# State-space stage of a one-core kernel: the step size is folded into the x rows on GpSimd, the chunk's four weighted gram products become one, and a third convolution tile moves from TensorE to ScalarE and VectorE taps

## The chip, the cores and the metric

One Trainium2 chip, one core of it. The metric is the device time of one execution in microseconds (us), measured on that core; lower is better. The engines are TensorE (PE, its weight loads PEld), VectorE (DVE), ScalarE (ACT), GpSimd (POOL) and the DMA queue (SP).

## What is computed

Eight sequences of 512 rows of 128 numbers go through an attention block, a mixture of 16 experts, a state-space block, and the experts again. The change lies in the state-space block, whose core is:

```python
zxbcdt = einsum('bld,ed->ble', u, W_in)            # z, x, B, C, dt
dt = softplus(dt + dt_bias)
conv = conv_b
for w in range(4):                                 # causal, per channel
    conv = conv + xp[:, w:w + L, :] * conv_w[:, w]
xBC = silu(conv)                                   # 512 channels: x (256), B (128), C (128)
dtx = dt[..., None] * x
h = h * exp(dt * A) + outer(dtx, B)                # step by step over the 512 rows
y = h @ C + x * D
g = y * silu(z); g = g * rsqrt(mean(g * g) + eps) * norm_w
out = g @ W_out.T
```

## The kernel before, in words

The program is written by hand: each engine has its own instruction list, and counting semaphores (`M["..."]` for this block) order them. Around the block lie the attention stage, the first expert stage and, behind it, the second expert stage; they are not changed except for a few set-up instructions.

The recurrence is done in chunks: a sequence (batch b, eight of them) has four chunks c of 128 rows. For a chunk, `front` on PE makes the product of B and C rows (bank 0), transposes x and B to row order (bank 1), and sums the log decays (bank 2). ACT copies bank 1 to `xb_tok` (`xb_out`) and exponentiates bank 2 into `segs` (`seg_exp`: four heads of 128x128). DVE (`grams`) masks the product into `cb`, multiplies the last column of `segs` by the step size (`to_end`), and makes for each of the four heads `gram` = segs * dt * cb. PE (`back`) adds into bank 3 the skip term, the term of the carried state, and gram times `xb_tok`; then it makes the chunk's state from `xw`, the x rows weighted by `to_end` on POOL (`weigh`). DVE takes y from bank 3 (`ys`), POOL gates it (`gate`), ACT squares it (`square`), POOL makes the scale (`rms`, two small operations), DVE applies it (`norms`), and PE transposes it (`g_turn`) through bank 5, which ACT empties (`gT_out`).

The next batch's inputs are made in between: `u_turn` and `u_low`, then the projections with the causal convolution of width 4. The 512 channels are four tiles. Two of them (`DVE_TILES`, B and C) are projected once on PE (`project_in`), ACT makes the first tap with the bias (`conv_first`), and DVE adds three taps (`conv_taps_of`), each one pass over 128x511 and fewer elements. The other two (`PE_TILES`, x) are convolved on PE: `conv` runs the split product for each of four shifts, 12 matmuls of 512 columns, against weights that hold the taps (`tapT`). ACT copies out the first of these (`conv_out`) and applies silu to the second straight from PSUM (`xs_last`). The banks are few: bank 7 holds, in turn, the turned rows, tile 0's projection, the first convolution, and the second half of z. `softplus` on DVE is a chain of 15 small operations on 128x16 numbers, which ends with `dt_a`, the step sizes and their products with A.

A step of `skew_pairs` does batch i's chunks (`second`), batch i+1's inputs (`first`), the output projection of batch i-1 (`third`), and parts of the router of batch i-2 (`fourth`). There are nine steps, from -1 (inputs only) to 7 (no inputs). Each engine's order in a step is written out by hand, for instance on DVE:

```python
            def step(i, odd, first, second, third, fourth):
...
                if second:
                    states(i, 1)
                    ys(i, odd, 1)
...
                    grams(i, odd, 2)
                if first:
                    softplus(i + 1, 1 - odd)
                if second:
                    ys(i, odd, 2)
```

An engine takes its instructions in this order and no other, so a wait at the head of one holds all that stand behind it.

## Time and profile before

| | us |
|---|---|
| median of 3 runs | 880.06 |
| lowest and highest run | 880.0, 883.94 |
| the profiled execution, its own time | 880.15 |
| its span in the trace | 878.4 |
| TensorE busy | 783.9 |
| VectorE busy | 670.9 |
| ScalarE busy | 552.8 |
| GpSimd busy | 215.9 |
| the nine steps of the state-space block | about 354.75 to 669.93 |

The span runs from the first to the last instruction in the trace; the device time has 1.7 us around it. Busy times are sums over all stages, and the stages have different limits: a step of the state-space block takes 37.6 to 38.8 us, of which PE is busy about 32 and DVE about 29, so no engine is full there, and which wait ends last has to be read in the step.

### The profile page before, as it was taken

The numbers are of one execution on the slowest core, as the hardware profiler recorded it, in microseconds if no ns is written. First come the engines' busy times: TensorE is split into PE (matmuls) and PEld (weight loads), VectorE is DVE, ScalarE is ACT, GpSimd is POOL, SyncE is SP. The second block draws the span as 40 slices with busy tenths as digits, with TensorE's granted clock in tenths as the row PEclk, the third lists the DMA queues.
The fourth block names the chain that finished last, engine by engine and source line by source line (L and its number), as shares of the span: only waits on it lengthen the run. The fifth ranks groups of instructions, "written<-read, shape, count | busy, mean of one in ns | idle before, by whom it ended". The sixth has DMA issues, their size and how long they took to land.

```text
span 878.4 us, 14762 instructions
## 1 busy us (share of the span) xinstructions
PE 783.9 (89%) x3912; PEld 617.2 (70%) x3912; DVE 670.9 (76%) x1610; ACT 552.8 (63%) x934; POOL 215.9 (25%) x383
## 2 busy tenths in 40 slices
PE   6879997999999999687888979798887899999998
PEld 4656775777777877566776867676665677777776
DVE  3488887878888888585777878687756988888886
ACT  4565656777778776635545363554624877777784
POOL 2235454001000000133545454464534100000000
PEclk9999999899999999998999999999987999999999
DMA  8000002545555452000000000000003445556552
GB/s 229 1 1 3 4 2 86 173 160 181 181 173 182 172 170 72 1 0 1 1 1 2 2 3 1 3 0 2 2 1 122 168 171 185 182 190 194 186 176 69
DMA packets 28113, 75.87 MB, mean 86 GB/s; under 512 B 4323, under 2 KB 8862, under 8 KB 28062
## 3 DMA queue, kind: packets, MB, share of 16 engines
q1 hardware_dynamic: 27908, 75.30, 25.8%
q8 instruction: 19, 0.31, 0.1%
q14 instruction: 32, 0.26, 0.1%
q10 hardware_dynamic: 154, 0.00, 0.0%
HBM read 72.66 MB, written 2.62 MB: 86 GB/s over the span
## 4 chain that ended last, share of the span: by engine, by line
PE 56%; DVE 15%; issue 14%; ACT 6%; POOL 6%; DMA 1%; DVEq 0%; POOLq 0%; SPq 0%; ACTq 0%
PE ps L1442 7%; PE ps L1461 7%; PE ps L1462 6%; PE ps L1463 6%; PE ps L1443 6%; PE ps L1444 6%; DVE conv_acc L1112 3%; PE ps L1613 3%; POOL rt_small L389 2%; PE ps L1439 2%; PE ps L1297 2%; DVE gram L1167 1%; DVE xn L1057 1%; DVE t L911 1%; POOL g L483 1%
## 5 line engine op out<-in xcount | busy, mean ns | idle before, releaser
L684 ACT ACTIVATE s_ring<-ps,b1T 128x512 f32<-128x512 f32 x256 | 172.8, 688 | 85.7 <-PE ps L1463 84.6
L1072 DVE SCALAR_TENSOR_TENSOR s_ring<-s_ring,top_col,r_all 128x1024 f32<-128x1024 f32 x128 | 165.6, 1294 | 64.2 <-ACT s_ring L684 60.1
L1038 DVE TENSOR_TENSOR s_lo<-s_ring,s_hi 128x1024 fp32r<-128x1024 f32 x128 | 156.1, 1219 | 0.0
L672 ACT ACTIVATE s_hi<-s_ring 128x1024 fp32r<-128x1024 f32 x128 | 134.4, 1050 | 1.4 <-DVE s_ring L1072 1.4
L1461 PE MATMUL ps<-ffn_hi,w_hi 128*128 (+1 forms) x256 | 104.8, 409 | 2.0 <-issue 2.0
L1442 PE MATMUL ps<-s_hi,w_hi 128*128 128x512 f32 x256 | 103.4, 404 | 1.4 <-DVE s_lo L1038 1.4
L1462 PE MATMUL ps<-ffn_lo,w_hi 128*128 (+1 forms) x256 | 102.3, 400 | 0.0
L1463 PE MATMUL ps<-ffn_hi,w_lo 128*128 (+1 forms) x256 | 102.3, 400 | 0.0
L1443 PE MATMUL ps<-s_lo,w_hi 128*128 128x512 f32 x256 | 101.4, 396 | 0.0
L1444 PE MATMUL ps<-s_hi,w_lo 128*128 128x512 f32 x256 | 101.3, 396 | 0.0
L457 POOL TENSOR_TENSOR ramp<-upto,dt_a 128x512 f32<-128x512 f32 x32 | 33.4, 1046 | 156.7 <-DVE dt_a L1153 156.7
L1442 PEld LDWEIGHTS ps<-s_hi,w_hi 128*128 128x128 f32 x256 | 48.1, 188 | 25.6 <-issue 12.1
L1461 PEld LDWEIGHTS ps<-ffn_hi,w_hi 128*128 128x128 f32 x256 | 49.2, 192 | 12.7 <-issue 2.3
L1463 PEld LDWEIGHTS ps<-ffn_hi,w_lo 128*128 128x128 f32 x256 | 48.8, 191 | 12.1
L1462 PEld LDWEIGHTS ps<-ffn_lo,w_hi 128*128 128x128 f32 x256 | 48.9, 191 | 10.8
L1444 PEld LDWEIGHTS ps<-s_hi,w_lo 128*128 128x128 f32 x256 | 48.1, 188 | 11.6
L1443 PEld LDWEIGHTS ps<-s_lo,w_hi 128*128 128x128 f32 x256 | 48.2, 188 | 10.5
L483 POOL TENSOR_TENSOR g<-y,zs 128x256 f32<-128x256 f32 x32 | 23.7, 741 | 124.7 <-DVE y L1195 63.0
L1112 DVE SCALAR_TENSOR_TENSOR conv_acc<-ps,conv_taps,conv_acc 128x511 f32<-128x511 f32 (+2 forms) x48 | 35.2, 748 | 10.3 <-ACT conv_acc L714 9.1
L1167 DVE SCALAR_TENSOR_TENSOR gram<-segs,dt_a,cb 128x128 f32<-128x128 f32 x128 | 39.5, 369 | 0.1
L911 DVE TENSOR_SCALAR t<-X,rt_mv,rt_small 128x128 f32<-128x128 f32 (+1 forms) x64 | 31.3, 549 | 8.7 <-POOL rt_small L404 8.7
L1578 PEld LDWEIGHTS ps<-xb_tok,gram 128*128 128x128 f32 x256 | 33.9, 197 | 2.3 <-DVE gram L1167 1.1
(232 smaller groups left out, 1602.3 us busy)
## 6 DMA issues: line engine op xcount, KB each, us to landing
r_all<-route_dram SPq DMA_DIRECT2D x128, 512.0 KB, 3.7
out_dram<-X SPq DMA_DIRECT2D x8, 256.0 KB, 4.1
X<-in_L_attn_a_x_dram SPq DMA_DIRECT2D x1, 1792.0 KB, 9.4
w_rows<-in_L_ffn_mlp_w_dram SPq DMA_DIRECT2D x1, 1024.0 KB, 12.6
route_dram<-route_cols SPq DMA_DIRECT2D x64, 8.0 KB, 1.4
route_rows<-route_dram SPq DMA_DIRECT2D x16, 32.0 KB, 3.4
in_rows<-in_L_attn_b_W_in_dram SPq DMA_DIRECT2D x1, 384.0 KB
X<-in_L_attn_a_x_dram SPq DMA_DIRECT2D x1, 256.0 KB, 2.6
```

What stands on the lines that cost most here:

```text
L672: eng.activation(s_hi[:, q % NR, :, :], s_ring[:, q % NR, :, :], ACT.Copy).then_inc(F["hi"], 1)
L684: eng.activation(s_ring[:, q % NR, e % 2, :], bank(e % 4), ACT.Silu, bias=b1T[:, e:e + 1], scale=ALPHA).then_inc(F["act"], 1)
L1038: eng.tensor_tensor(s_lo[:, q % NR, :, :], s_ring[:, q % NR, :, :], s_hi[:, q % NR, :, :].bitcast(F32), ALU.subtract).then_inc(F["lo"], 1)
L1072: eng.scalar_tensor_tensor(out=s_ring[:, q % NR, :, :], in0=s_ring[:, q % NR, :, :], scalar=top_col[:, 0:1], in1=r_all[:, q % NR, :, :], o ...
L1112: eng.scalar_tensor_tensor(out=conv_acc[:, j, s:], in0=bank(7 - k)[:, 0:SEQ - s], scalar=conv_taps[:, j, CONV_W - 1 - s:CONV_W - s], in1=c ...
L1167: eng.scalar_tensor_tensor(out=gram[:, c % 2, h, :], in0=segs[:, c % 2, h, :], scalar=dt_a[:, par, 0, c, h:h + 1], in1=cb[:, c % 2, :], op ...
L1442: eng.matmul(bank(6), w2_hi[:, e, :], hi, start=False, stop=False)
L1443: eng.matmul(bank(6), w2_hi[:, e, :], lo, start=False, stop=False)
L1444: mm = eng.matmul(bank(6), w2_lo[:, e, :], hi, start=False, stop=(e == NE - 1))
L1461: eng.matmul(bank(e % 4), w1_hi[:, e, :], ffn_hi[:, b, :], start=True, stop=False)
L1462: eng.matmul(bank(e % 4), w1_hi[:, e, :], ffn_lo[:, b, :], start=False, stop=False)
L1463: eng.matmul(bank(e % 4), w1_lo[:, e, :], ffn_hi[:, b, :], start=False, stop=True).then_inc(F["h"], 1)
```

## The change

Three things are changed.

First, the step size is multiplied into the x rows: POOL makes `xdt` = xb_tok * dt for every chunk (`step_x`, one more POOL operation per chunk, placed ahead of `weigh` or, for the last chunk, behind `gate` of the third), and `xw` is made from `xdt` and the last column of `segs`. `to_end` is gone.

Second, `gram` no longer holds dt, so that DVE makes the four heads in one product of 128x512, with `cb` repeated over the heads. PE multiplies it with `xdt`, for which it now waits.

Third, `PE_TILES` is `(1,)` and `DVE_TILES` is `(2, 3, 0)`: the first x tile is projected once on PE into bank 7 (where `conv(0)` stood), ACT makes its first tap (where `conv_out` stood), and DVE its three other taps, between `grams` of the third chunk and `softplus`. The second half of z, which uses bank 7 next, waits for them. In the set-up, one tap tile less and one projection tile more is turned and split.

```diff
-PE_TILES = (0, 1)
-DVE_TILES = (2, 3)
+PE_TILES = (1,)
+DVE_TILES = (2, 3, 0)
+TILE_BANK = (7, 6, 7)
...
+            def step_x(b, par, c):
+                n = NT * b + c
+                wait(eng, M["xb"], n + 1)
+                wait(eng, M["dt"], b + 1)
+                wait(eng, M["y_ps"], n - 1)
+                wait(eng, M["xw"], (NT - 1) * b + max(c - 1, 0))
+                eng.tensor_tensor(xdt[:, c % 2, :].rearrange("s (h p) -> s h p", h=NH),
+                                  xb_tok[:, c % 2, 0:2, :].rearrange("s j (h p) -> s (j h) p", p=HD),
+                                  dt_a[:, par, 0, c, :].unsqueeze(2).to_broadcast([P, NH, HD]),
+                                  ALU.mult).then_inc(M["xdt"], 1)
...
                 if second:
                     gate(i, odd, 1)
                     rms(i, 1)
+                    step_x(i, odd, 2)
                     weigh(i, odd, 2)
                     gate(i, odd, 2)
+                    step_x(i, odd, 3)
                 if first:
                     ramps(i + 1, 1 - odd, 0)
...
             def grams(b, par, c):
...
-                for h in range(NH):
-                    eng.scalar_tensor_tensor(out=gram[:, c % 2, h, :], in0=segs[:, c % 2, h, :],
-                                             scalar=dt_a[:, par, 0, c, h:h + 1], in1=cb[:, c % 2, :], op0=ALU.mult,
-                                             op1=ALU.mult).then_inc(M["gram"], 1)
+                eng.tensor_tensor(gram[:, c % 2, :, :], segs[:, c % 2, :, :],
+                                  cb[:, c % 2, :].unsqueeze(1).to_broadcast([P, NH, P]), ALU.mult).then_inc(M["gram"], 1)
...
                 if first:
+                    conv_taps_of(i + 1, 2)
                     softplus(i + 1, 1 - odd)
...
             def z_proj(b, k):
                 if k == 0:
-                    wait(eng, M["conv"], 6 * b + 6)
+                    wait(eng, M["conv"], 9 * b + 6)
                 else:
-                    wait(eng, M["raw"], b + 1)
+                    wait(eng, M["conv"], 9 * b + 9)
...
-                wait(eng, M["gram"], NH * (n + 1))
+                wait(eng, M["xdt"], n + 1)
+                wait(eng, M["gram"], n + 1)
                 for h in range(NH):
                     mm = eng.matmul(bank(3)[:, h * HD:(h + 1) * HD], gram[:, c % 2, h, :],
-                                    xb_tok[:, c % 2, h // 2, (h % 2) * HD:(h % 2 + 1) * HD], start=False, stop=(h == NH - 1),
+                                    xdt[:, c % 2, h * HD:(h + 1) * HD], start=False, stop=(h == NH - 1),
                                     skip_group_check=True)
...
                 if first:
-                    conv(i + 1, 0)
+                    project_in(i + 1, 2)
```

How the instructions stand on VectorE in the middle of a step, from the third chunk's gram to the same chunk's y, before (`dt_tmp` and `dt_a` are softplus):

```order
L1159 TENSOR_TENSOR cb<-ps,upto 128x128
L1162 TENSOR_TENSOR to_end<-segs,dt_a 128x4
L1167 SCALAR_TENSOR_TENSOR gram<-segs,dt_a,cb 128x128 x4
L1138 TENSOR_SCALAR dt_tmp<-dt_tmp 128x16
L1139 RECIPROCAL dt_tmp<-dt_tmp 128x16
```

and after the change, at the same place:

```order
L1170 TENSOR_TENSOR cb<-ps,upto 128x128
L1174 TENSOR_TENSOR gram<-segs,cb 128x512
L1123 SCALAR_TENSOR_TENSOR conv_acc<-ps,conv_taps,conv_acc 128x511
L1123 SCALAR_TENSOR_TENSOR conv_acc<-ps,conv_taps,conv_acc 128x510
L1123 SCALAR_TENSOR_TENSOR conv_acc<-ps,conv_taps,conv_acc 128x509
L1149 TENSOR_SCALAR dt_tmp<-dt_tmp 128x16
L1150 RECIPROCAL dt_tmp<-dt_tmp 128x16
```

Five instructions of the gram have become one, and three whole-row taps now stand ahead of softplus and of all that follows it, the third chunk's y among them.

GpSimd from the second chunk's gate to the next batch's first ramp, before:

```order
L483 TENSOR_TENSOR g<-y,zs 128x256
L488 TENSOR_TENSOR g_rs<-g_ss,eps 128x1
...
L491 TENSOR_TENSOR g_rs<-g_rs,mhalf 128x1
...
L467 TENSOR_TENSOR xw<-xb_tok,to_end 128x256
...
L473 TENSOR_TENSOR state_d<-state,decay 128x256
L483 TENSOR_TENSOR g<-y,zs 128x256
...
L457 TENSOR_TENSOR ramp<-upto,dt_a 128x512
```

and after:

```order
L495 TENSOR_TENSOR g<-y,zs 128x256
L500 TENSOR_TENSOR g_rs<-g_ss,eps 128x1
...
L503 TENSOR_TENSOR g_rs<-g_rs,mhalf 128x1
...
L468 TENSOR_TENSOR xdt<-xb_tok,dt_a 128x256
L479 TENSOR_TENSOR xw<-xdt,segs 128x256
...
L485 TENSOR_TENSOR state_d<-state,decay 128x256
L495 TENSOR_TENSOR g<-y,zs 128x256
...
L468 TENSOR_TENSOR xdt<-xb_tok,dt_a 128x256
...
L458 TENSOR_TENSOR ramp<-upto,dt_a 128x512
```

The third chunk's `xdt`, for which PE waits, stands behind the second chunk's gate and rms, and the fourth chunk's behind the third chunk's gate.

## Rows read from the trace of the kernel before

**Rows 1.** The page, part 1: busy us of the engines.

```profile
PE 783.9 (89%) x3912; PEld 617.2 (70%) x3912; DVE 670.9 (76%) x1610; ACT 552.8 (63%) x934; POOL 215.9 (25%) x383
```

**Rows 2.** Windows: busy us per engine, granted clock; three steps, one piece.

```profile
479.24:518.08 38.84, 33.76 (x188) 28.18 (x188) 29.09 (x110) 19.58 (x41) 18.26 (x34) 0.91 0.01 2
518.08:555.84 37.76, 31.96 (x187) 26.51 (x188) 29.40 (x110) 19.51 (x41) 19.36 (x34) 1.00 0.01 3
594.19:631.75 37.56, 31.97 (x188) 26.55 (x188) 29.03 (x108) 19.43 (x41) 18.86 (x34) 1.00 0.01 1
...
511.10:514.50 3.40, 3.40 (x9) 2.59 (x9) 2.28 (x17) 3.01 (x4) 2.85 (x9) 0.51 0.00 0
```

**Rows 3.** Timeline of TensorE, step 4: start, us, line, tiles, count [idle before].

```profile
538.93 0.47 PE L1490 MATMUL ps<-uT,tapT 128*128 128x512 f32 x1
...
541.80 0.61 PE L1570 MATMUL ps<-skip_diag,xs 128*128 128x128 f32 x4
542.68 1.00 PE L1578 MATMUL ps<-xb_tok,gram 128*128 128x64 f32 x8
548.59 0.41 PE L1603 MATMUL ps<-ident,gn 128*128 128x128 f32 x2 [1.37 <-ACT gT L794]
555.25 0.30 PE L1358 MATMUL ps<-ident,rt_w 128*128 128x128 f32 x1 [1.07 <-ACT gT L794]
```

**Rows 4.** Timeline of VectorE, step 4.

```profile
522.43 1.82 DVE L1057 TENSOR_SCALAR xn<-X,ln_mv,ln_rs 128x128 f32 x4
...
532.57 4.54 DVE L1112 SCALAR_TENSOR_TENSOR conv_acc<-ps,conv_taps,conv_acc 128x511 f32<-128x511 f32 x6 [1.23 <-ACT conv_acc L714]
...
540.30 1.13 DVE L1167 SCALAR_TENSOR_TENSOR gram<-segs,dt_a,cb 128x128 f32<-128x128 f32 x4
541.35 0.16 DVE L1138 TENSOR_SCALAR dt_tmp<-dt_tmp 128x16 f32<-128x16 f32 x1
545.24 0.17 DVE L1153 TENSOR_TENSOR dt_a<-dt_a,neg_A 128x16 f32<-128x16 f32 x1
```

**Rows 5.** Timeline of ScalarE and GpSimd, step 4.

```profile
531.76 0.78 ACT L714 ACTIVATE conv_acc<-ps,cols,conv_taps 128x512 f32<-128x512 f32 x1 [5.37 <-PE ps L1492]
539.62 0.74 POOL L483 TENSOR_TENSOR g<-y,zs 128x256 f32<-128x256 f32 x1 [3.06 <-DVE y L1195]
540.47 0.42 ACT L787 ACTIVATE g_sq<-g 128x256 f32<-128x256 f32 x1 [2.56 <-POOL g L483]
541.41 0.55 POOL L491 TENSOR_TENSOR g_rs<-g_rs,mhalf 128x1 f32<-128x1 f32 x1 [0.16 <-POOL g_rs L488]
541.92 0.61 POOL L467 TENSOR_TENSOR xw<-xb_tok,to_end 128x256 f32<-128x256 f32 x1
546.29 0.78 POOL L483 TENSOR_TENSOR g<-y,zs 128x256 f32<-128x256 f32 x1 [3.19 <-DVE y L1195]
548.07 0.37 ACT L794 ACTIVATE gT<-ps 128x256 f32<-128x256 f32 x1
```

**Rows 6.** Grouped instructions: prices of one two-input VectorE product.

```profile
L1038 DVE TENSOR_TENSOR s_lo<-s_ring,s_hi 128x1024 fp32r<-128x1024 f32 x128 | 156.1, 1219 | 0.0
L1205 DVE TENSOR_TENSOR X<-ps,X 128x512 f32<-128x512 f32 x4 | 2.8, 692 | 8.5 <-PE ps L1613 8.5
```

**Rows 7.** Timeline of VectorE: grams beside GpSimd work, and xn behind it.

```profile
372.83 2.28 DVE L1167 SCALAR_TENSOR_TENSOR gram<-segs,dt_a,cb 128x128 f32<-128x128 f32 x4
...
446.14 2.14 DVE L1057 TENSOR_SCALAR xn<-X,ln_mv,ln_rs 128x128 f32<-128x128 f32 x4 [0.17 <-POOL ln_rs L451]
```

**Rows 8.** Timeline of step -1: VectorE's softplus, first and last.

```profile
361.69 0.18 DVE L1138 TENSOR_SCALAR dt_tmp<-dt_tmp 128x16 f32<-128x16 f32 x1 [0.28 <-ACT dt_tmp L754]
364.70 0.18 DVE L1153 TENSOR_TENSOR dt_a<-dt_a,neg_A 128x16 f32<-128x16 f32 x1
```

**Rows 9.** Timeline of the last step, third chunk: GpSimd and TensorE.

```profile
650.96 0.54 POOL L491 TENSOR_TENSOR g_rs<-g_rs,mhalf 128x1 f32<-128x1 f32 x1
651.15 1.97 PE L1578 MATMUL ps<-xb_tok,gram 128*128 128x64 f32 x8 [0.73 <-DVE gram L1167]
```

**Rows 10.** Timeline of the set-up: TensorE's wait behind it.

```profile
55.98 3.67 PE L1297 MATMUL ps<-xnT,qT 128*128 128x512 f32 x8 [1.35 <-DVE dtT L1013]
```

More of the change, by code:

```diff
@@ L155, in build @@
             xb_tok = own("xb_tok", [P, 2, 3, P])
-            to_end = own("to_end", [P, 2, NH])
+            xdt = own("xdt", [P, 2, DI])
             xw = own("xw", [P, 2, DI])
@@ L224, in build @@
         M = {n: sem("ssm_" + n) for n in (
-            "stats", "aggr", "rstd", "xn", "uT_ps", "uT", "u_lo", "cv_ps", "tap", "conv", "raw", "xs", "z_ps",
+            "stats", "aggr", "rstd", "xn", "uT_ps", "uT", "u_lo", "cv_ps", "tap", "conv", "xs", "z_ps",
             "z_raw", "zs", "dt_ps", "dt_x", "dt_m", "dt_u", "log", "dt", "a", "dk_ps", "decay", "ramp", "cb_ps", "cb",
-            "xb_ps", "xb", "seg_ps", "segs", "gram", "end", "xw", "st_ps", "state_d", "state", "y_ps", "y_off", "y",
+            "xb_ps", "xb", "seg_ps", "segs", "gram", "xdt", "xw", "st_ps", "state_d", "state", "y_ps", "y_off", "y",
             "g", "sq", "rms", "gn", "gT_ps", "gT", "o_ps", "x")}
@@ L463, in weigh @@
                 k = (NT - 1) * b + c
-                wait(eng, M["xb"], n + 1)
+                wait(eng, M["xdt"], n + 1)
+                wait(eng, M["segs"], n + 1)
                 wait(eng, M["st_ps"], k - 1)
-                wait(eng, M["end"], n + 1)
                 eng.tensor_tensor(xw[:, c % 2, :].rearrange("s (h p) -> s h p", h=NH),
-                                  xb_tok[:, c % 2, 0:2, :].rearrange("s j (h p) -> s (j h) p", p=HD),
-                                  to_end[:, c % 2, :].unsqueeze(2).to_broadcast([P, NH, HD]),
+                                  xdt[:, c % 2, :].rearrange("s (h p) -> s h p", h=NH),
+                                  segs[:, c % 2, :, P - 1:P].to_broadcast([P, NH, HD]),
                                   ALU.mult).then_inc(M["xw"], 1)
@@ L713, in conv_first @@
                 wait(eng, M["xs"], 3 * b)
[L714 removed]
+                eng.activation(conv_acc[:, j, :], bank(TILE_BANK[k]), ACT.Identity, bias=conv_bias[:, j:j + 1],
                                scale=conv_taps[:, j, CONV_W - 1:CONV_W]).then_inc(M["tap"], 1)
[L717 to L721 removed]
             def xs_silu(b, par):
[L724 to L725 removed]
+                wait(eng, M["conv"], 9 * b + 9)
                 wait(eng, M["y_ps"], NT * (b - 1))
[L727 removed]
+                for first, count in ((DVE_TILES[2], 1), (DVE_TILES[0], 2)):
                     eng.activation(xs[:, par, first:first + count, :], conv_acc[:, first:first + count, :],
@@ L767, in xb_out @@
                 wait(eng, M["xb_ps"], n + 1)
-                wait(eng, M["y_ps"], n - 1)
+                wait(eng, M["xdt"], n - 1)
                 wait(eng, M["st_ps"], k)
-                wait(eng, M["xw"], k)
                 eng.activation(xb_tok[:, c % 2, :, :], bank(1)[:, 0:3 * P].rearrange("t (j c) -> t j c", j=3),
@@ L776, in seg_exp @@
                 wait(eng, M["seg_ps"], n + 1)
-                wait(eng, M["gram"], NH * (n - 1))
-                wait(eng, M["end"], n - 1)
+                wait(eng, M["gram"], n - 1)
+                wait(eng, M["xw"], (NT - 1) * b + max(c - 1, 0))
                 eng.activation(segs[:, c % 2, :, :], bank(2).rearrange("s (h t) -> s h t", h=NH),
@@ L1109, in conv_taps_of @@
                 j = DVE_TILES[k]
-                wait(eng, M["tap"], 2 * b + k + 1)
+                wait(eng, M["tap"], 3 * b + k + 1)
                 for s in range(1, CONV_W):
-                    eng.scalar_tensor_tensor(out=conv_acc[:, j, s:], in0=bank(7 - k)[:, 0:SEQ - s],
+                    eng.scalar_tensor_tensor(out=conv_acc[:, j, s:], in0=bank(TILE_BANK[k])[:, 0:SEQ - s],
                                              scalar=conv_taps[:, j, CONV_W - 1 - s:CONV_W - s], in1=conv_acc[:, j, s:],
@@ L1115, in conv_taps_of @@
                     if s < CONV_W - 1:
[L1116 removed]
+                        wait(eng, M["conv"], 9 * b + 3 * k + s)
             def dt_arg(b):
@@ L1146, in softplus @@
                 link(eng.tensor_scalar(x_, x_, 0.0, None, ALU.max))
-                wait(eng, M["gram"], NH * NT * (b - 1))
+                wait(eng, M["xdt"], NT * (b - 1))
                 wait(eng, M["ramp"], NT * (b - 1))
@@ L1405, in expert_weights_2 @@
                     mm.then_inc(prep3_ps, 1)
+                eng.transpose(bank(1)[:, 0:P], in_rows[:, 2 + DVE_TILES[2], :], ident[:, :])
                 for k, j in enumerate((2 + DVE_TILES[0], 2 + DVE_TILES[1], 0, 1)):
```

50 lines of the change are left out of this document (22 added, 28 removed).

## The prediction

> **What bounds the kernel now.** I read the page first. By its busy sums TensorE is the fullest engine and VectorE the second [rows 1]. Such a sum is an average over stages, so I cut the state-space block into steps, each from one batch's first `front` on PE to the next one's: a step takes 37.6 to 38.8 us, with PE busy about 32 and DVE about 29 [rows 2]. Neither is full. So I went through the timeline of one step whose clock was full throughout (step 4, 518.08 to 555.84) and asked at each idle spell of PE what ended it.
>
> In its second half PE waits for two things: 1.37 us ahead of the transpose `g_turn(1)` at 548.59 and 1.07 us ahead of the router transpose at 555.25, both ended by ACT's copy out of bank 5 [rows 3]. The first of these hangs on a chain that begins on DVE: gram of the third chunk (540.30), softplus (541.35 to the end of `dt_a` at 545.41), then the third chunk's y [rows 4], its gate on POOL (546.29), its square and a z copy on ACT, and ACT's `gT` copy at 548.07 [rows 5]. DVE has no gap of more than 0.25 us from 540.30 to that y. So the middle of a step is set by DVE's order of work, and PE has room beside it.
>
> **The change, part by part**, in step 4's times.
>
> *PE loses a convolution.* The first of its 12 matmuls starts at 538.93 and what follows starts at 541.80 [rows 3]: 2.87 us. Three matmuls of the same size take their place, a quarter of that, 0.72. PE could be 2.15 us earlier at `back(2)`. But there it now needs `xdt(2)`, and POOL makes it behind gate and rms of the second chunk. That gate starts at 539.62 because y came then, the square follows at 540.47, rms ends at 541.96, and the next slot on POOL is at 541.92, where `xw` (same shape) takes 0.61 [rows 5]. So `xdt(2)` is ready at 542.53 and the gram matmuls start at about 542.6; before, they started at 542.68 [rows 3]. The wait for POOL takes the place of the convolution. Gain on PE: 0.1, and it is not on the chain anyway.
>
> *DVE gets three taps ahead of softplus.* They need ACT's first tap, which stands behind the square (0.42, with its small read 0.51, from 540.47): it starts at 540.98 and takes 0.78 [rows 5], so DVE starts at 541.78. Six taps take 4.54 us [rows 4], three take 2.27, with the short gaps of a dependent chain 2.3. Softplus starts at 544.0 in place of 541.35: +2.65. Half of this is the taps' wait for ACT, and the shorter gram does not help, for it would have ended earlier still.
>
> *Softplus gets shorter.* In step 4 it takes 4.06 us (541.35 to 545.41); in step -1, where POOL does nothing, 3.19 (361.69 to 364.88) [rows 4, 8]. The difference, 0.87, lies beside POOL's `xw` and `state_d`, which will be over by 543.8, before the later softplus begins. I take -0.75 of it (0 to -0.87).
>
> *One gram product for five instructions.* A product of 128x1024 from SBUF takes 1.219, of 128x512 with one PSUM input 0.692 [rows 6]; half of the first is 0.61, so the new one costs 0.61 to 0.69. I take 0.69. Before, `to_end` and four products take 1.13 plus 0.13. So 0.55 to 0.6 less, four times a step. Where it counts: the first chunk's gram stands ahead of `xn` (522.43), for which PE waits. There up to 0.65 is won; nothing in steps where `xn` waited for POOL's `ln_rs` instead, as at 446.14 [rows 4, 7]; and `xn`, 1.8 to 2.1 us beside POOL's work, gets an `xdt` more beside it. I take -0.3 (+0.3 to -0.65). The second chunk's gram lies beside the output projection on PE, the third's now ends in the wait for the tap, the fourth's stands ahead of the router's exp on ACT, worth 0 to 0.45; I take -0.1, because `xdt(3)` pushes POOL's ramp beside it, and a gram beside POOL products took 2.28 instead of 1.13 [rows 4, 7]. The Trainium skill says the same in "GPSIMD Engine Reference", Key points: GpSimd shares its SBUF interfaces with VectorE and contends with instructions that have two SBUF inputs. By that rule the taps, with one input in PSUM, stay at their length and the wide gram is the one at risk; if all four collided, a step would cost 1.9 instead of 1.5.
>
> *Sum for a step:* +2.65 - 0.75 - 0.3 - 0.1 = +1.5. All that hangs on the third chunk's y (gate, square, `gT`, `g_turn(1)`, the last convolution, then `front` of the next step) moves with it. Bounds: 2.65 - 0.87 - 0.65 - 0.45 = +0.7, and 2.65 + 0.3 = +2.95, of which I take 2.5 as the edge, since softplus surely loses part of its slow rows. Seven steps (0 to 6) have both chunks and inputs: **+10.5** (4.9 to 17.5).
>
> *Step -1* has no chunks to hide beside. Softplus started at 361.69, right behind dt's exp on ACT [rows 8]. Now ACT's first tap (0.78) and three taps (2.3) come between: **+3.1** (2.8 to 3.2), and ACT's silu chain and the first `front` follow it.
>
> *Last step:* no taps. Its third chunk's gram matmuls waited for DVE until 651.15; rms ended at 651.50, `xdt(2)` is ready at 652.1 [rows 9]: +1.0, less 0.3 from the first gram. **+0.7** (-0.5 to +2).
>
> *The clock.* The matmuls of the last convolution ran at the lower level (0.51 of full, 1.2 GHz) in 511.10 to 514.50, and that step took 38.84, against 37.76 and 37.56 for two at full clock (2.4 GHz) [rows 2]: about 1 us. PE had then waited for `g_turn(1)` just before. This wait was 1.37 in step 4; now PE finishes z about 0.7 earlier and goes on at `g_turn(1)` 1.6 later, so it grows to some 3.7 us, at the same place. Four steps that ran this stretch at full clock can fall: 0 to 4. I take **+2**.
>
> *Set-up:* four transposes and two copies of a tap tile less, one of each more, of which PE waited 1.35 at the end [rows 10]: **-0.4** (0 to -0.8).
>
> Sum: 10.5 + 3.1 + 0.7 + 2 - 0.4 = +15.9. Against the profiled execution's own 880.15 (span 878.4) this is **896**; the median of the runs, 880.06, is the same within 0.1.
>
> **Rivals.**
>
> *Faster, TensorE decides.* If PE's own work set the step, eight convolutions shortened by 2.15 would give -17.2, 863 us. For it: PE is at 89% [rows 1]. Against it: the 1.37 us of idleness ended by `gT` [rows 3]. It decides from the point where softplus could start 2.65 later without y being late; there is no gap on DVE for that. The Trainium skill, "Perfetto Trace Analysis", Identifying the Most-Contended Engine, would have the engine with the highest occupancy optimized first, which by busy time is PE and speaks for this rival, though it adds that PE's headroom be judged by weight loads, and these are at 70%, under DVE's 76%. Chance 0.05.
>
> *No change, the grams pay for the taps.* DVE's busy time hardly changes: 4 x 0.57 less, 2.3 more. If every gram's saving reached the chain and softplus lost all its slow rows, a step would gain 2.28 + 0.87 against 2.65, and with step -1 the time would be 880 to 883. Against it: two of the four grams lie beside longer work. Chance 0.08.
>
> *Much slower: POOL or the clock comes on top.* POOL gets four products more in a step, 2.4 us, and goes through the router's chain with no gap; the fourth chunk's gate follows. If steps cost their upper 2.5, and the clock 4, the time is 880.15 + 17.5 + 3.1 + 4 + 1 = 906. For it: the collision rows [rows 7]. Chance 0.15.
>
> *My forecast:* 0.72, its own range 889 to 902.
>
> **How the numbers follow.** What a measurement of this kernel can tell from no change is about 0.5%, 4.4 us. Faster than 876: the first rival and a sliver of the second, 0.06. Within: 0.07. Slower than 884.5: 0.87. The range that leaves out 2 in 10 goes from the forecast's lower bounds (4.9 + 2.8 - 0.5 = +7.2, 887) to well into the much slower case, 904.
>
> **What the next profile would show.** Right: DVE idle about 1.4 us behind the third gram, ended by ACT's first tap, then three taps of 0.75; PE waiting some 2 us in `back(2)` for `xdt` on POOL, and over 3 us ahead of `g_turn(1)`; steps of 39 to 40 us; step -1 longer by 3.1; gram at 0.61 to 0.69. Wrong: steps under 38 us, or `g_turn(1)` no later against the step's start than before. What would make it wrong most easily is ACT reaching the first tap earlier than the square allows, which its order excludes, or a wide gram that is blocked by POOL in every step.

## The result, and the profile after

| | before | after |
|---|---|---|
| median, us (4 runs each, same chip) | 882.0 | 908.36 |
| lowest and highest, us | 880.0, 885.96 | 905.96, 908.7 |
| ratio of the times, 95% interval | | 1.0291 (1.0256 to 1.0327) |
| the profiled execution, its own time and span | 880.15, 878.4 | 908.7, 907.0 |

The change makes the kernel 2.9% slower, some 25.6 us. The direction was forecast (896 us), the size was not: the time lies outside the range of 887 to 904.

The page's first part, then the windows of the changed kernel: step -1 from `u_turn` to the first `front`, steps 3, 4 and 6, and a piece in the last convolution of step 4 (columns: window, us, busy us and instructions of PE, PEld, DVE, ACT, POOL, granted clock of PE, DMA share, GB/s).

```profile
PE 790.8 (87%) x3837; PEld 617.9 (68%) x3837; DVE 668.9 (74%) x1506; ACT 552.7 (61%) x934; POOL 242.2 (27%) x414
```

```profile
353.11:376.58 23.47, 14.45 (x58) 11.33 (x56) 11.38 (x30) 11.65 (x17) 2.04 (x2) 0.71 0.00 0
494.37:535.49 41.12, 32.63 (x179) 26.89 (x179) 29.02 (x99) 19.25 (x41) 21.26 (x38) 0.92 0.01 2
535.49:576.91 41.42, 31.74 (x179) 25.94 (x179) 29.10 (x98) 19.77 (x41) 22.23 (x38) 0.92 0.01 2
617.82:659.18 41.36, 33.55 (x179) 27.38 (x179) 28.92 (x97) 19.62 (x41) 21.78 (x38) 0.88 0.00 1
570.20:573.20 3.00, 3.00 (x9) 2.33 (x8) 1.59 (x9) 2.99 (x5) 2.61 (x6) 0.51 0.02 5
```

Steps 2 to 6 are 41 to 43 us long, not 39 to 40, and no step has the full clock that three of the steps before had [rows 2]. TensorE has 75 matmuls fewer and is busy 7 us longer: it has less to do and does it more slowly. Now TensorE's timeline in step 4 (start, us, line, tiles, count, and in brackets the idle time ahead and what ended it):

```profile
542.21 0.95 PE L1509 MATMUL ps<-ident,xn 128*128 128x128 f32 x4 [2.24 <-DVE xn L1068]
558.20 0.60 PE L1582 MATMUL ps<-state,xs 128*128 128x256 f32 x2
560.63 1.10 PE L1587 MATMUL ps<-xdt,gram 128*128 128x64 f32 x8 [1.84 <-POOL xdt L468]
568.60 0.41 PE L1612 MATMUL ps<-ident,gn 128*128 128x128 f32 x2 [3.32 <-ACT gT L803]
570.62 0.63 PE L1499 MATMUL ps<-uT,tapT 128*128 128x512 f32 x1
573.41 0.40 PE L1500 MATMUL ps<-uT,tapT 128*128 128x512 f32 x1
576.31 0.30 PE L1365 MATMUL ps<-ident,rt_w 128*128 128x128 f32 x1 [0.56 <-ACT gT L803]
```

The wait ahead of `g_turn(1)` was 1.37 us [rows 3] and is 3.32; right behind it the same convolution matmul takes 0.63 us at half clock and 0.40 at the end, at full clock. Step 4 does not stand for all steps, as the same place in step 5 shows:

```profile
603.48 1.64 PE L1587 MATMUL ps<-xdt,gram 128*128 128x64 f32 x8 [1.84 <-POOL xdt L468]
604.91 1.17 PE L1600 MATMUL ps<-xw,xb_tok 128*128 128x256 f32 x2
611.22 0.41 PE L1612 MATMUL ps<-ident,gn 128*128 128x128 f32 x2 [1.44 <-ACT gT L803]
612.15 0.40 PE L1499 MATMUL ps<-uT,tapT 128*128 128x512 f32 x1
```

Here the half clock comes behind the wait for `xdt(2)` (1.64 us for the gram matmuls instead of 1.10, 1.17 for the two of the state instead of 0.65), the wait ahead of `g_turn(1)` is 1.44 and the last convolution has the full clock. Over the seven full steps of this execution the half clock comes at three places: around `u_turn` in six steps (three before), behind the wait for `xdt(2)` in steps 0, 1, 5 and 6 (none before), and in the last convolution in steps 2, 3, 4 and 6 (0, 1 and 3 before). VectorE (its first row is the third tile's taps in step -1) and GpSimd in the same step:

```profile
363.60 2.32 DVE L1123 SCALAR_TENSOR_TENSOR conv_acc<-ps,conv_taps,conv_acc 128x511 f32<-128x511 f32 x3 [0.95 <-ACT conv_acc L731]
...
539.63 2.44 DVE L1068 TENSOR_SCALAR xn<-X,ln_mv,ln_rs 128x128 f32 x4 [0.65 <-POOL ln_rs L452]
...
558.01 0.93 DVE L1174 TENSOR_TENSOR gram<-segs,cb 128x512 f32<-128x512 f32 x1
559.72 2.32 DVE L1123 SCALAR_TENSOR_TENSOR conv_acc<-ps,conv_taps,conv_acc 128x511 f32<-128x511 f32 x3 [0.78 <-ACT conv_acc L731]
561.96 0.17 DVE L1149 TENSOR_SCALAR dt_tmp<-dt_tmp 128x16 f32<-128x16 f32 x1
...
565.26 0.17 DVE L1164 TENSOR_TENSOR dt_a<-dt_a,neg_A 128x16 f32<-128x16 f32 x1
```

```profile
539.57 0.61 POOL L468 TENSOR_TENSOR xdt<-xb_tok,dt_a 128x256 f32<-128x256 f32 x1
540.34 0.66 POOL L479 TENSOR_TENSOR xw<-xdt,segs 128x256 f32<-128x256 f32 x1 [0.16 <-POOL xdt L468]
540.96 1.03 POOL L458 TENSOR_TENSOR ramp<-upto,dt_a 128x512 f32<-128x512 f32 x1
559.96 0.61 POOL L468 TENSOR_TENSOR xdt<-xb_tok,dt_a 128x256 f32<-128x256 f32 x1
```

Taps, softplus (3.47 us) and the wait for `xdt(2)` stand where the prediction put them. What it had not: `xn` takes 2.44 us instead of 1.82 [rows 4], with three GpSimd products beside it.

Where the 28.6 us between the two spans lie: 1.3 ahead of step -1 (`u_turn` at 353.11 instead of 351.85), 4.9 in step -1, 21.3 in the seven full steps, 1.0 in the last step, 0.1 behind it. For the comparisons below each full step is cut in three at TensorE: from the first `front` to `u_turn`, to `g_turn(1)`, and to the next `front`. The numbers are means of the seven steps in us, worked out from the start times in one profiled execution of each kernel; the ratios are those of all runs.

| kernel | front to u_turn | to g_turn(1) | to front | step | clock | ratio to before, 95% |
|---|---|---|---|---|---|---|
| before | 6.52 | 23.63 | 7.19 | 37.33 | 0.96 | 1 |
| after | 6.80 | 26.03 | 7.54 | 40.37 | 0.89 | 1.0291 (1.0256 to 1.0327) |
| e1_fold | 6.89 | 23.62 | 6.33 | 36.84 | 0.98 | 0.9972 (0.9947 to 0.9996) |
| e2_taps | 6.55 | 25.54 | 8.74 | 40.83 | 0.89 | 1.0346 (1.0317 to 1.0374) |
| e3_hold | 5.42 | 25.52 | 6.82 | 37.75 | 0.95 | 1.0117 (1.0074 to 1.0160) |
| b_hold | 5.46 | 23.77 | 6.84 | 36.07 | 0.99 | 0.9911 (0.9870 to 0.9951) |
| e5_fill | 6.86 | 26.08 | 6.26 | 39.19 | 0.96 | 1.0223 (1.0183 to 1.0262) |
| e7_late | 6.88 | 25.04 | 8.23 | 40.15 | 0.90 | 1.0234 (1.0198 to 1.0270) |
| e8_best | 5.45 | 23.60 | 6.32 | 35.37 | 1.00 | 0.9881 (0.9843 to 0.9918) |
| e9_early | 6.84 | 25.81 | 8.20 | 40.84 | 0.90 | 1.0350 (1.0302 to 1.0399) |
| e10_late_hold | 5.40 | 23.63 | 8.34 | 37.37 | 0.95 | 1.0132 (1.0082 to 1.0182) |
| e11_keep | 6.96 | 25.38 | 7.77 | 40.11 | 0.94 | 1.0258 (1.0212 to 1.0304) |
| e12_keep_hold | 5.55 | 25.47 | 7.35 | 38.38 | 0.97 | 1.0171 (1.0131 to 1.0211) |
| e13_onetap | 5.50 | 24.98 | 6.32 | 36.80 | 0.97 | 1.0043 (1.0013 to 1.0072) |
| e14_full | 6.75 | 25.50 | 6.41 | 38.67 | 0.99 | 1.0176 (1.0142 to 1.0210) |
| b_fill | 6.48 | 23.65 | 6.53 | 36.66 | 1.00 | 0.9958 (0.9939 to 0.9978) |
| e16_first | 6.87 | 25.20 | 6.76 | 38.84 | 0.92 | 1.0212 (1.0169 to 1.0256) |
| e17_combo | 5.55 | 24.84 | 8.36 | 38.75 | 0.93 | 1.0166 (1.0133 to 1.0199) |
| e18_hold_first | 5.44 | 25.09 | 6.32 | 36.85 | 0.97 | 1.0073 (1.0052 to 1.0094) |
| e19_all | 5.83 | 24.73 | 6.41 | 36.96 | 0.99 | 1.0034 (1.0010 to 1.0059) |

In the profiled executions the stretch ahead of step -1 ends anywhere from 351.9 to 357.9 us, whatever the kernel, so small effects are read from the steps and the ratios, not from spans. A difference between two ratios is uncertain by some 3 to 5 us, as their intervals show.

### The profile page after: what moved, and what is told of

Its sections match the earlier page's. It is cut to its first block, busy times and chain, and to the rows that moved or that the text cites. A ratio compares the mean times of both kernels' runs of the same rounds, so it can differ in the third digit from the quotient of the medians.

```text
span 907.0 us, 14564 instructions
## 1 busy us (share of the span) xinstructions
PE 790.8 (87%) x3837; PEld 617.9 (68%) x3837; DVE 668.9 (74%) x1506; ACT 552.7 (61%) x934; POOL 242.2 (27%) x414
## 4 chain that ended last, share of the span: by engine, by line
PE 32%; issue 8%; DVE 7%; POOL 5%; ACT 2%; POOLq 0%; DVEq 0%; ACTq 0%
PE ps L1450 3%; PE ps L1469 3%; PE ps L1470 3%; PE ps L1471 3%; PE ps L1451 3%; PE ps L1452 3%; PE ps L1622 3%; DVE conv_acc L1123 2%; POOL g L495 1%; DVE xn L1068 1%; PE ps L1587 1%; PE ps L1498 1%; PE ps L1500 1%; PE ps L1499 1%; PE ps L1447 1%
## 5 line engine op out<-in xcount | busy, mean ns | idle before, releaser
L1123 DVE SCALAR_TENSOR_TENSOR conv_acc<-ps,conv_taps,conv_acc 128x511 f32<-128x511 f32 (+2 forms) x72 | 53.2, 748 | 17.3 <-ACT conv_acc L731 15.6
L1587 PE MATMUL ps<-xdt,gram 128*128 128x64 f32 x256 | 36.6, 291 | 14.1 <-POOL xdt L468 14.1
L1587 PEld LDWEIGHTS ps<-xdt,gram 128*128 128x128 f32 x256 | 36.0, 211 | 18.1 <-POOL xdt L468 17.3
L731 ACT ACTIVATE conv_acc<-ps,cols,conv_taps 128x512 f32<-128x512 f32 x24 | 18.4, 769 | 37.9 <-PE ps L1500 37.9
```

The lines of the kernel that those rows point to most:

```text
L1123: eng.scalar_tensor_tensor(out=conv_acc[:, j, s:], in0=bank(TILE_BANK[k])[:, 0:SEQ - s], scalar=conv_taps[:, j, CONV_W - 1 - s:CONV_W - s] ...
L1587: mm = eng.matmul(bank(3)[:, h * HD:(h + 1) * HD], gram[:, c % 2, h, :], xdt[:, c % 2, h * HD:(h + 1) * HD], start=False, stop=(h == NH - ...
```

## The experiments

**The two halves of the change.** The kernel before with the fold alone (e1_fold: `step_x` and one gram product, `PE_TILES` as before), and with the third tile's taps alone (e2_taps):

```diff
-PE_TILES = (0, 1)
-DVE_TILES = (2, 3)
+PE_TILES = (1,)
+DVE_TILES = (2, 3, 0)
...
                 if first:
+                    conv_taps_of(i + 1, 2)
                     softplus(i + 1, 1 - odd)
```

The diff is that of e2_taps; e1_fold has all of the change but these lines and what hangs on them.

> The kernel before with the fold alone: the step size goes into the x rows on GpSimd, and a chunk has one gram product on VectorE; the third convolution tile stays on TensorE. Theory A (VectorE's third-tile taps ahead of softplus set the later step, and the fold only takes its gain and loses some of it beside xn): 877 to 883 us, u_turn to g_turn(1) shorter than or as long as before, xn near 2.4 us instead of 1.82. Rival B (the wait of TensorE for the scaled x rows, or GpSimd's work, makes the steps later): 890 us or more. Either way the granted clock of steps 4 to 6 stays 1.00 if it is the missing convolution work that lowers it.

> The kernel before with the third convolution tile on ScalarE and VectorE taps alone; the step size stays in the gram, with two products on VectorE. Theory A: 901 to 908 us, since softplus comes 2.7 us later in each step and 2.9 us later in step -1, with steps granted less than 0.95 of the clock. Rival B (the fold is the larger part): 890 us or less.

Measured: 0.9972 and 1.0346. The fold costs nothing and wins a quarter of a per cent; the taps are the whole loss, and more than I expected (901 to 908 was asked for, 914.9 came). In e1_fold, with all of the convolution work, steps 5 and 6 still had only 0.96 and 0.95 of the clock (step 4 had 1.00), behind the wait for `xn`, so the clock does not need the missing work to fall. Rival B, that GpSimd's rows and TensorE's wait for them make the step later, falls: without the fold there is no such wait, and the kernel is slower. In e2_taps the last part of a step takes 8.74 us instead of 7.19, in a kernel whose convolution there has the same 12 matmuls, and TensorE runs this convolution at half clock in all seven steps, behind waits of 3.8 to 4.1 us: the first sign that the clock is worth more than 2 us.

**GpSimd kept away from xn.** The changed kernel, and the kernel before, with one wait more on GpSimd:

```diff
                 if first:
                     ssm_norm(i + 1)
+                    wait(eng, M["xn"], NT * (i + 1) + NT)
                 if second:
```

> The changed kernel with one wait more: GpSimd starts a chunk's scaled x rows (and the two operations behind them) only when VectorE has finished xn. Theory A with the failed term (GpSimd's rows beside xn and ln_rs cost 0.8 to 1.0 us per step): 899 to 903 us, xn back near 1.8 us. Rival (the extra wait makes the scaled x rows late for TensorE, or xn was not what decided front0 to u_turn): 908 us or more.

> The kernel before with the same wait of GpSimd for xn. By theory A's reading of xn (1.82 us beside GpSimd, less when alone) about 0.75 us per step less, 873 to 877 us. Rival (xn's length is its own and GpSimd's operations only move to beside something else): 880 to 884 us.

Measured: 1.0117 (15 us less than the change; 899 to 903 us were expected, 5 to 9 less) and 0.9911 (7.8 us less than before; 877.3 us, at the slow edge of the 873 to 877 expected). VectorE's `xn`, and GpSimd's next product, in e3_hold:

```profile
530.66 1.11 DVE L1069 TENSOR_SCALAR xn<-X,ln_mv,ln_rs 128x128 f32 x4 [0.65 <-POOL ln_rs L452]
```

```profile
532.10 0.66 POOL L468 TENSOR_TENSOR xdt<-xb_tok,dt_a 128x256 f32<-128x256 f32 x1 [1.47 <-ACT xb_tok L781]
```

`xn` alone takes 1.11 us, 2.44 beside GpSimd. That is 1.3 us a step, and front to `u_turn` falls by 1.4. The rest comes with the clock, which rises from 0.89 to 0.95: the last part of a step falls by 0.72, the middle by 0.51, though neither was touched. TensorE waits less for `xn` (0.91 us in step 4, 2.24 in the change), and no step has the half clock at `u_turn` any more.

**TensorE kept busy in its waits.** Products that nothing reads, ahead of `u_turn` and of `g_turn(1)`:

```diff
+            def fill(at, count):
+                for _ in range(count):
+                    eng.matmul(bank(at), tapT[:, 0, 0, 0, :], uT[:, 0, PAD:PAD + SEQ], start=True, stop=True)
...
+                    if second:
+                        wait(eng, M["z_raw"], 2 * (i + 1))
+                        fill(7, 4)
                     u_turn(i + 1)
...
                     z_proj(i + 1, 1)
+                    wait(eng, M["z_raw"], 2 * (i + 1) + 1)
+                    fill(6, 10)
```

> The changed kernel with extra products of 128 x 512 on TensorE that nothing reads: 4 of them ahead of u_turn and 10 ahead of g_turn(1), where TensorE waits. If the clock at half level is what is left over the forecast (theory): the granted clock of the seven steps rises from 0.85 to 0.92 to 0.95 or more and the time falls by 7 to 10 us, to 898 to 902 us, though TensorE does more work. Rival (the steps end by VectorE and GpSimd, and a slower TensorE is only hidden): 906 to 912 us, whatever the clock.

Measured: 1.0223, 6 us less with 14 matmuls more in each step; 902.7 us is just over the 898 to 902 expected, and the clock of 0.96 is as expected. The convolution at the end of step 4 ran at full clock:

```profile
565.84 2.54 PE L1632 MATMUL ps<-uT,tapT 128*128 128x512 f32 x10
568.22 0.38 PE L1612 MATMUL ps<-ident,gn 128*128 128x128 f32 x2
568.80 0.48 PE L1498 MATMUL ps<-uT,tapT 128*128 128x512 f32 x1
569.12 0.39 PE L1499 MATMUL ps<-uT,tapT 128*128 128x512 f32 x1
```

The first two rows show why it was not more: `g_turn(1)` starts the moment the ten products end, with no wait left. They seem to have been too many: the part up to `g_turn(1)` takes 26.08 us here and 25.50 in e14_full below, where 6 stand in place of the 10 (and 12 more in another wait).

**Taps behind softplus.**

```diff
                 if first:
-                    conv_taps_of(i + 1, 2)
                     softplus(i + 1, 1 - odd)
                 if second:
                     ys(i, odd, 2)
                     norms(i, 1)
                     states(i, 2)
+                if first:
+                    conv_taps_of(i + 1, 2)
```

`z_proj(1)` and `z_out(1)`, which need the tile's bank, move behind `decay_sums` and `decays`; e10_late_hold has the wait for `xn` as well.

> The changed kernel with the third tile's VectorE taps moved behind ys(2), norms(1) and states(2), so that softplus goes first, and z_proj(1) and z_out(1) moved behind the decays. Theory A (the taps ahead of softplus set the step): u_turn to g_turn(1) falls from 26.0 to about 23.5 us per step, and the time by 13 to 20 us, to 888 to 895 us. Rival (the taps cost the same wherever they stand, because VectorE is full, or xs comes later instead): 904 us or more.

> The changed kernel with the third tile's VectorE taps behind ys(2), norms(1) and states(2) (z_proj(1) and z_out(1) behind the decays) and with the wait of GpSimd for xn. If the late taps alone gave back only 6 us because the clock was at half level where z_proj(0) and the convolution ran (theory), then with the clock up by the wait u_turn to g_turn(1) is 24.0 us or less and the time 884 to 890 us. Rival (late taps only push z_proj(1) and the convolution back, whatever the clock): 892 to 896 us, as the changed kernel with the wait alone.

Measured: 1.0234 and 1.0132, both misses on the time. The middle part does fall, to 25.04, and with the wait for `xn` to 23.63, that of the kernel before. That fits taps that set `g_turn(1)`, but does not prove it, since `z_proj(1)` and `z_out(1)` left the middle part as well. What is won there is lost behind it: the last part rises to 8.2 and 8.3 us, where `z_proj(1)` now stands ahead of the convolution and `z_out(1)` ahead of silu. The clock is not the reason: step 4 of e10_late_hold has 1.00 of it, and its last part takes 9.62 us. For e10 the rival was right: late taps only push work back.

**The rows of chunk 2 early.** On GpSimd, in the changed kernel:

```diff
                 if second:
+                    step_x(i, odd, 2)
                     gate(i, odd, 1)
                     rms(i, 1)
-                    step_x(i, odd, 2)
```

> The changed kernel with the scaled x rows of chunk 2 ahead of gate(1) and rms(1) on GpSimd. Rival B (TensorE's wait for the rows of chunk 2 is on the path): the wait of 1.84 us goes and the time falls by 5 us or more. Theory A: the wait goes or becomes a wait for something else, and the time stays within 3 us of 908, since VectorE's taps and softplus end y(2) anyway; gate(1) and rms(1) come 0.6 us later.

Measured: 1.0350, 5 us slower than the change, which is at the edge of what the intervals can tell. TensorE's wait for `xdt(2)` is gone, and came back in another place, as TensorE's row for `g_turn(1)` shows (step 4):

```profile
572.71 0.41 PE L1612 MATMUL ps<-ident,gn 128*128 128x128 f32 x2 [4.15 <-ACT gT L803]
```

Two waits of 1.84 and 3.32 us became one of 4.15, right ahead of the convolution, and the step's last part rose from 7.54 to 8.20: the convolution now runs at half clock in all seven steps, and the stretch of it behind `xdt(2)` is gone. Rival B is refuted a second time, and my bound of 3 us was too tight.

**The missing products, or the waits?** TensorE does the removed convolution again, into a bank that is free then, and nobody reads it (e11_keep), also with the wait for `xn` (e12_keep_hold):

```diff
                 if first:
                     project_in(i + 1, 2)
+                    wait(eng, M["conv"], 9 * (i + 1) + 6)
+                    for s in range(CONV_W):
+                        product(bank(6), parts_of(tapT, 0, CONV_W - 1 - s, slice(None)),
+                                parts_of(uT, slice(PAD - s, PAD - s + SEQ)), s == 0, s == CONV_W - 1)
```

> The changed kernel in which TensorE still does the third tile's 12 convolution products in every step, behind project_in(2) and into the bank that conv uses later, and nothing reads them. Theory (what goes beyond the forecast is the clock, which the missing products let fall): granted clock of the seven steps back to 0.95 or more from 0.90, time 897 to 901 us although TensorE has 3 us more to do in each step. Rival (the clock falls by the waits that the change brings, not by the missing products, or it costs nothing): 906 us or more.

> Both: the discarded 12 products and the wait of GpSimd for xn, in the changed kernel. If the wait's 14 us were 9 to 10 us of its own and the rest clock, the products have little clock left to give back and this comes within 3 us of the wait alone, 891 to 897 us, at a clock of 0.96 or more. Rival (the two give their gains apart): 886 us or less.

Measured: 1.0258 and 1.0171. The products alone give back 3 us of the 9 expected, which the intervals cannot tell from nothing, and on top of the wait for `xn` they give nothing (1.0117 without them, intervals that overlap). TensorE in step 4 of e11_keep:

```profile
566.71 0.41 PE L1612 MATMUL ps<-ident,gn 128*128 128x128 f32 x2 [2.73 <-ACT gT L803]
568.34 0.63 PE L1500 MATMUL ps<-uT,tapT 128*128 128x512 f32 x1
```

The work is all there, and the convolution behind the wait of 2.73 us still runs at half clock. So the missing products are not what lowers the clock there. They do matter at another place: with them the wait for `xdt(2)` is filled, no step has the half clock behind it, and the mean clock rises from 0.89 to 0.94. But the time hardly follows, because TensorE only reaches the wait ahead of `g_turn(1)` earlier. e12_keep_hold shows this exchange best. In e3_hold five of the seven steps have the half clock behind `xdt(2)`, the wait ahead of `g_turn(1)` is then 1.35 to 1.68 us, and the convolution has the full clock in these five. In e12_keep_hold none has it behind `xdt(2)`, the wait ahead of `g_turn(1)` is 2.2 to 3.0 us, and four convolutions run at half clock, at a mean clock that is higher (0.97 against 0.95). The length of that wait does not decide alone, either: in e11_keep the same 2.51 us stands ahead of a slow convolution in step 3 and of one at full clock in step 5.

**All waits filled, and the control.** The kept products, 4 ahead of `u_turn`, and 6 instead of 10 ahead of `g_turn(1)` (e14_full); the 4 and 6 in the kernel before (b_fill).

> The changed kernel with all three gaps of TensorE filled by products that nothing reads: 4 ahead of u_turn, the third tile's 12 behind project_in(2), and 6 ahead of g_turn(1). If the clock is the larger part of the excess over the forecast: the seven steps at 0.98 or more, front0 to u_turn 6.9, u_turn to g_turn(1) 25.5 and g_turn(1) to front0 6.3 us, together 12 us less than the changed kernel, 896 to 899 us. Rival (the fills delay what they stand ahead of, or the clock's part is small): 902 us or more.

> The kernel before with the same 4 and 6 products ahead of u_turn and g_turn(1), as a control. Its mean clock in the seven steps is 0.96 already, so there is little to win: 877 to 882 us if products in a wait cost nothing, with the wait of 1.37 us ahead of g_turn(1) nearly used up. Rival (products in the waits delay the transposes behind them): 884 us or more.

Measured: 1.0176, 897.3 us, and 0.9958, both inside what was expected. Steps 3 and 4 of e14_full:

```profile
487.64:526.36 38.72, 34.91 (x200) 28.86 (x201) 29.18 (x99) 19.23 (x41) 21.24 (x38) 1.00 0.01 2
526.36:566.69 40.33, 35.26 (x201) 29.46 (x201) 29.21 (x97) 19.72 (x41) 22.24 (x38) 0.96 0.01 2
```

With 22 matmuls more in a step than the changed kernel has, it is 10 us faster (1.0291 less 1.0176, times 880). In the kernel before the same costs nothing and gives 3.7 us. So the half clock costs the change 6.4 us over what it costs the kernel before, if the fills cost nothing of their own; by the intervals this is uncertain by some 5 us, and the steps of the traces say 7 (1.70 us a step given back here, 0.67 there). By parts of the step, the last convolution's part gives back 1.13 us here and 0.66 there, the middle part 0.53 here and nothing there: of the 7 us about 3 lie behind `g_turn(1)` and 4 ahead of it. At the clock of 0.99 and 1.00 a step of the change is 2.0 us longer than one of b_fill (38.67 against 36.66).

**One tap instead of three**, with the wait for `xn` (the third tile's convolution then lacks two shifts):

> The changed kernel with the wait of GpSimd for xn and only one of the third tile's three VectorE taps; the oldest two are left out, so the convolution of that tile is another. 1.55 us less of VectorE's time ahead of softplus. Theory A (VectorE's work ahead of softplus goes to the step one for one): 1.55 us less in each of seven steps and step -1, 12.4 us, 880 to 884 us. Rival (VectorE's idle time or another wait takes up part): 888 us or more.

Measured: 1.0043, 6.5 us less than e3_hold, half of what one for one would give. VectorE's taps and the third chunk's y in e3_hold, then ScalarE's copy for `g_turn(1)`:

```profile
549.42 2.32 DVE L1124 SCALAR_TENSOR_TENSOR conv_acc<-ps,conv_taps,conv_acc 128x511 f32<-128x511 f32 x3 [0.77 <-ACT conv_acc L732]
555.50 0.42 DVE L1202 TENSOR_TENSOR y<-ps,y_off 128x256 f32<-128x256 f32 x1
557.78 0.37 ACT L804 ACTIVATE gT<-ps 128x256 f32<-128x256 f32 x1
```

and the same in e13_onetap, with the copy of z that now stands ahead of the square:

```profile
542.36 0.75 DVE L1124 SCALAR_TENSOR_TENSOR conv_acc<-ps,conv_taps,conv_acc 128x511 f32<-128x511 f32 x1 [0.84 <-ACT conv_acc L732]
547.41 0.42 DVE L1207 TENSOR_TENSOR y<-ps,y_off 128x256 f32<-128x256 f32 x1
```

```profile
548.82 0.60 ACT L751 ACTIVATE zs<-ps 128x512 f32<-128x512 f32 x1
549.32 0.41 ACT L797 ACTIVATE g_sq<-g 128x256 f32<-128x256 f32 x1
550.19 0.39 ACT L804 ACTIVATE gT<-ps 128x256 f32<-128x256 f32 x1
```

From the first tap to y: 6.08 us, then 5.05. Of 1.57 us taken away 1.03 arrives, since softplus moves back beside GpSimd's products and takes 3.96 instead of 3.47. From y to the copy: 2.28, then 2.78. The square waits behind z, which is late because TensorE's `front(3)` is. In both kernels TensorE runs from the wait for `xdt(2)` to this `front(3)` at half clock (the gram matmuls of chunk 2 take 1.49 and 1.53 us, 1.00 before [rows 3]), so this wait is probably part of what makes z late, though no run here tests it. So 0.5 of 1.57 us reaches `g_turn(1)` in this step. A second chain, TensorE to ScalarE, ends barely ahead of VectorE's: theory A's one for one was wrong.

**ScalarE's first tap earlier, and the sums.** `conv_first(2)` ahead of `square(1)` (e16_first); this, the wait for `xn` and the early rows of chunk 2 (e17_combo); without the early rows (e18_hold_first); and with all fills (e19_all):

```diff
+                if first:
+                    conv_first(i + 1, 2)
                 if second:
                     square(i, 1)
-                if first:
-                    conv_first(i + 1, 2)
```

> The changed kernel with conv_first(2) ahead of square(1) on ScalarE. VectorE's idle 0.78 us ahead of the third taps is a wait for conv_first(2), which stands behind square(1), which waits for GpSimd's gate(1). If VectorE decides: 0.78 us less in seven steps and a little in each step's clock, 5 to 8 us, 900 to 903 us. Rival (ScalarE's queue behind front(3) decides, and it waits for the scaled x rows): 906 us or more.

> The changed kernel with three moves: GpSimd waits for xn, conv_first(2) ahead of square(1) on ScalarE, and the scaled x rows of chunk 2 ahead of gate(1) on GpSimd. With conv_first(2) no longer behind gate(1) the early rows cost nothing, and both chains that meet at g_turn(1) are shorter: 883 to 888 us, 6 to 11 us under the wait alone. Rival (the early rows cost here too, as they did alone): 894 us or more.

> The changed kernel with GpSimd's wait for xn and with conv_first(2) ahead of square(1), the rows of chunk 2 where the change put them. If the early rows alone spoilt the three moves (theory): the two gains of 14 and 7 us add but for the clock that both count, 884 to 890 us. Rival (the two moves do not add, whatever the rows): 893 us or more.

> The changed kernel with GpSimd's wait for xn, conv_first(2) ahead of square(1) and all three fills (4, 12 and 6 products that nothing reads). By the pieces measured so far a step is front0 to u_turn 5.5, u_turn to g_turn(1) 24.8 and g_turn(1) to front0 6.4 us, 36.7 us, 0.6 less than in the kernel before, and step -1 is 3 us longer: 878 to 884 us. Rival (the fills delay the transposes once the waits that they fill are short): 888 us or more.

Measured: 1.0212, 1.0166, 1.0073 and 1.0034. VectorE's 0.78 us of idle time was real and on the path: 7 us less. The combination missed its forecast by 9 us. Its waits again lie in one place, 3.27 us ahead of `g_turn(1)` in step 4, its convolution runs at half clock in all seven steps, and its last part takes 8.36 us; without the early rows the convolution has the full clock throughout, that part is 6.32 and the time 890.0, the upper end of what I expected. With everything, the third tile on taps comes within 0.3% of the kernel before, 2 us above my range for it: `front` to `u_turn` takes 5.83 and not the 5.5 of its pieces.

**The better kernel.** e1_fold with the wait for `xn` (e8_best):

> The kernel before with the fold alone and with the wait of GpSimd for xn. If the two gains add (0.9972 and 0.9911): ratio 0.988, 872 us. The fold puts more of GpSimd's work beside xn than the kernel before has, so the wait may be worth more here: down to 868 us. Rival (the scaled x rows come later and TensorE waits for them): 878 us or more.

Measured: 0.9881 (0.9843 to 0.9918), 871.1 us. The gains add, the clock is 1.00 in all seven steps, and it beats both kernels.

## Why the prediction was right in direction and wrong in size

What failed is the clock term, and with it the small term for the first gram and `xn`, whose sign was wrong. At nearly equal, full clock the change costs 1.0176 less 0.9958, 19.2 us (some 3.5 either way); the prediction without its clock term had 13.9. The other 6.4 are the clock, against the 2 that were forecast. By its steps:

- **PE loses a convolution, and waits for `xdt(2)` instead.** Right: the wait is 1.84 us, "some 2 us" was asked for. The faster rival is dead. What was not foreseen is the half clock behind this wait, in four of seven steps, though it costs little there.
- **Taps ahead of softplus, +2.65, and softplus shorter, -0.75.** Right: `u_turn` to `g_turn(1)` is 1.85 longer at full clock (25.50 against 23.65), 1.9 was forecast. Softplus shrank by 0.59 instead of 0.75. DVE's gap is 0.78 and not 1.4, because the gram beside GpSimd takes 0.93 and not 0.69 and starts 0.4 later against `u_turn` than the gram's work did before; the tap starts within 0.1 us of where it was said to, once the 0.4 us of a later `u_turn` is taken off. The runs add what the sum did not see: a second chain is so near that this term is a cost one for one, but not a gain one for one.
- **First gram and `xn`, -0.3.** The sign was wrong. By e1_fold `front` to `u_turn` is 0.4 longer (6.89 against 6.52), since `xdt` adds to the GpSimd work beside `xn`. I had the row of 1.8 to 2.1 "beside POOL's work" and did not ask what it is alone: 1.10 to 1.11. **Fourth gram, -0.1:** nearer -0.4, from the last part of e8_best against b_hold in steps 4 to 6 (6.66 against 7.08, the clock full in both). Together the two terms are 0 and not -0.4, some 3 us in seven steps; a full-clock step came out at +2.0 instead of +1.5.
- **Step -1, +3.1.** The mechanism was right: from `u_turn` to the last operation of softplus it is 15.73 us, 12.85 before, +2.9 [rows 8]. The step as a whole is 4.9 longer; the other 2.0 come at a clock of 0.71 (1.00 before). That clock was anywhere from 0.65 to 0.92 in the other new kernels, b_hold and e8_best among them, so it is not the change's alone. At 0.85 (e14_full) against 0.92 (b_fill) the step is 3.1 longer, in one execution each.
- **Last step, +0.7.** 1.0.
- **The clock, +2 (0 to 4).** This is the step that failed most. I priced one place, the last convolution, as up to four steps that lose 1 us each, and put the rest of the step at nothing. The place is one of those where it falls, and the wait ahead of it was foreseen ("some 3.7 us", it is 3.0 to 3.3 in steps 2 to 4, though 1.2 to 1.7 in the others). The last convolution runs at half clock in four steps after and in three before, and by the fills this part costs some 3 us more than before: a little over the term, within its bounds. What was missing is some 4 us ahead of `g_turn(1)`. There the half clock comes at two places that the prediction did not have. One is behind the wait for `xn`, which the wrong sign above made longer (the four transposes of `u_turn` take 0.95 us at 542.21, in step 4 of e11_keep 0.65; with this wait shortened the clock went from 0.89 to 0.95). The other is behind the wait for `xdt(2)`. The rows point to the first: with the half clock behind `xdt(2)` in five steps (e3_hold) the middle part takes 25.52 us, with it in none (e12_keep_hold) 25.47. And half of the 4 us come from step 0, where the middle part takes 24.11 us in the change and 22.20 in e14_full: in the change the granted clock was 0.55 there from 381.90 to 389.50, with `u_turn` at 382.18, and 1.00 at that place in e14_full.
- **Set-up, -0.4.** Not to be told from the scatter of 6 us between executions.

The sum: 15.9, plus 4.4 for the clock, plus 3.5 for seven steps at +2.0 instead of +1.5, is 23.8 of the 25.6 measured; the last 1.8 is under what the intervals can tell. The much slower rival (906) named both the clock and GpSimd collisions, and was nearest, but the sum's own terms for collisions were on the grams. The Trainium skill, "GPSIMD Engine Reference", Key points, names two kinds of VectorE instruction that contend with GpSimd: those with two SBUF inputs and those in a 2-port mode. I had used only the first half. The trace fits the rule, if `xn` runs in such a mode, which the trace does not name: the one-input `xn` takes 2.44 instead of 1.11 us, the gram 0.93 where I took 0.69, while the three taps, which read PSUM, take 2.32 both in step 4 and in step -1, where GpSimd is idle.

What stays open: how much of e14_full's gain comes from each of its three fills, and why one wait is followed by the half clock and another of the same length is not.

## What to carry to other kernels

Ask of each wait of TensorE that a change lengthens or moves what runs right behind it: a wait ahead of a long run of matmuls that all else hangs on costs its own length and the half clock behind it, the same slowness ahead of another wait costs little, because that wait shrinks by it, and products that nothing reads, put into the wait, can be cheaper than nothing. Before counting an operation as fixed, look for a row where it runs alone; here one wait on another engine was worth more than the whole fold. And a chain that is made longer costs in full, but a chain made shorter pays only to the next one: taking two of VectorE's three taps away brought half of their time.

## What the runs showed of the hardware

A VectorE operation with one SBUF input and two scalars per row (`xn`, 128x128 x4) took 1.11 us alone and 2.44 us beside GpSimd's two-input products, more than twice as long. TensorE ran at half clock behind a wait of 2.73 us though 12 more matmuls of 512 columns had been issued earlier in the step (e11_keep, step 4), and at full clock when ten products filled the wait (e5_fill). A wait of 2.51 us was followed by the half clock in one step of e11_keep and by the full clock in another. The Trainium skill, "TensorE: Matmul & The Clock Gate", HAM oscillation, tells of kernels whose waits in every iteration let the clock fall each time; e9_early agrees with it, with the half clock in the last convolution of all seven steps, and e5_fill, where the filled wait leaves it in none; e11_keep has it in four of seven. The runs show besides that the place of the wait in the step decides what it costs.
